# A two-layer graph kernel: its first stage reads edges as joined records, turns the relation weights on TensorE, stores its tables earlier, and lays value and key rows out in 2048 bytes

## The chip, the cores and the metric

The kernel runs on one core of one Trainium2 chip. The metric is the device time of one execution in microseconds (us), lower is better; the number that counts is the median of several runs without the profiler.

## What is computed

Two layers of a graph network over 6250 nodes with 256 features and 200000 edges, sorted by their destination. Cut to what matters here:

```python
# layer 0: attention over the edges of each destination node, 4 heads of 64
enh = x + 0.1 * query_emb
Q, K, V = enh @ Wq + bq, enh @ Wk + bk, enh @ Wv + bv
scores = einsum(Q[dst], K[src] + 0.2 * rel_w[edge_type_64]) / 8      # per head
w = softmax of scores over the edges of each dst
x1 = layernorm(x + layernorm((sum of w * V[src]) @ Wo + bo + x) * gamma + beta)
# layer 1: six relation types
t = einsum('ni,rio->rno', x1, W) + b          # a row for each node and relation
agg[type_6, dst] += t[type_6, src]            # over the edges
out = layernorm(x1 + proj(mean of attention among the 6 rows of a node, + x1))
```

## The kernel before

There are four stages, each one a block of work on all engines, with a barrier behind the first two.

**First stage** (`prepare_phase`). Two things run side by side. TensorE and ScalarE make queries, keys and values for 49 tiles of 128 nodes: SyncE loads a tile of x (L679), TensorE turns it (L562), ScalarE adds the query embedding (L622), TensorE multiplies (L575 queries, L581 keys and values, L589 queries by relation weights), ScalarE copies the results out (L633, L641, L644, L650), SyncE stores the row of keys and values (L686) and the queries (L689), ScalarE's queue stores the relation part (L653). SyncE's queue is in a fixed order: the load of tile i, then the stores of tile i-2. Meanwhile VectorE works out tables of the edges: which edge each row of 128 edges begins with, for layer 0 (14 columns of 128 rows) and for layer 1 (15 columns). For this the edge arrays (src, dst, edge_type_6, edge_type_64) are first copied with padding to arrays in device memory (L666, L671). GpSimd then fetches, for each column, three times 128 rows of 128 numbers (L514, one indirect DMA each for src, dst and the type). TensorE's share of the tables is put between the tiles at fixed half-tile places (`of_tables`, with STARTS, SPREAD, RANGES, ROWS); TensorE waits there for VectorE. After the last tile SyncE's queue stores the tables (L696, L701, L702).

The relation weights are read transposed from device memory, number by number:

```python
for e in range(2):
    eng.dma_start(relc[HD * e:HD * e + HD, :], a["L0_gnn_rel_w"].rearrange("t d -> d t"),
                  allow_slow_non_contiguous=True).then_inc(w_in, 16)
```

A row of keys and values has 514 numbers (2056 bytes): 256 keys, and twice 128 values with a one behind them, whose product with the edge weights gives the softmax's denominator.

**Attention stage** (`attend_phase`). 440 units of 4 x 128 edges. For each, GpSimd gathers 4 x 128 rows of keys and values (L800) into one of 8 buffers; TensorE turns keys (L897), makes scores (L909, L912), turns the exponentials (L919) and sums values (L929). GpSimd waits for L929 of the unit 8 before, to have its buffer free. The indices come from VectorE (L1027), at the stage's start behind a setup of constants (L1099 to L1113).

**Update stage** (`update_phase`). For 49 tiles: the attention's sums and the node's own values are loaded, normalised, multiplied by Wo, added to x, normalised twice, and multiplied by the six relation matrices (L1313).

**Last stage** (`relate_mix_phase`). 1875 gathers of 128 rows of 1024 bytes (L1709), summed by one-hot products (L1740), then the attention among relations.

Of the kernel before, what the change touches and what calls it, by code (L numbers as in the profile page):

```python
# [10 lines left out]
I32 = mybir.dt.int32  # L24

# [9 lines left out]
HEADS = -(-E // 512)  # L35
FAR = 1 << 20
# [6 lines left out]
NQ = NB * P // WQ  # L43
K0 = -(-(E // C0 + NQ + 1) // 8) * 8
VP = 2 * HD + 1
KV = D + 2 * VP
# [63 lines left out]
def prepare_phase(nc, a, t):  # L110


    with ExitStack() as ctx:
        s = Scope(nc, ctx, "pre", give_back=True)
        src1 = s.sb("src1", [P, G1 * P], I32)
        row1 = s.sb("row1", [P, G1 * P])
        keep = s.sb("keep", [P, G1 * P])
        need = s.sb("need", [P, G1 * P], I32)
        ends = s.sb("ends", [P, NW], I32)
# [17 lines left out]
        pad_i = s.sb("pad_i", [2, EPAD - E], I32)  # L137
# [28 lines left out]
        rows_i = s.sb("rows_i", [P, G0, 3, P], I32)  # L166
# [3 lines left out]
        win = s.sb("win", [1, G0 * P])  # L170
        win_i = s.sb("win_i", [1, G0 * P], I32)
# [6 lines left out]
        relc = s.sb("relc", [P, R64])  # L178
# [14 lines left out]
        arrays_padded = s.sem("arrays_padded")  # L193
# [26 lines left out]
        names = ("src", "dst", "edge_type_6", "edge_type_64")  # L220
# [25 lines left out]
        with nc.Block() as block:  # L246
            @block.vector
            def _(eng):
# [50 lines left out]
                def tile_counts(L):  # L299
# [3 lines left out]
                    link(v.tensor_copy(srow[:, 0:P * GB[L]], p_b[:, 0:P * GB[L]]))  # L303
# [82 lines left out]
                def layer0_lists():  # L386
# [8 lines left out]
                    link(v.tensor_scalar(t.rneed0[:, :], win_i[:, :], 2, None, ALU.logical_shift_right))  # L395
                    link(v.tensor_scalar(t.rneed0[:, :], t.rneed0[:, :], 32.0, 32.0, ALU.mult, ALU.add))
# [18 lines left out]
                def make_rows(L, g):  # L415

                    rf = rows_f[g % 2]
                    eng.wait_ge(rows_in[g % G0], 48 * (1 + L + g // G0))
                    link(v.tensor_copy(rf[:, :, :], rows_i[:, g % G0, :, :]))
                    plan["read", L, g] = dve.n  # L420
                    link(v.tensor_scalar(rf[:, 1, :], rf[:, 1, :], rngneg[L][:, g:g + 1], None, ALU.add))
# [7 lines left out]
                    else:  # L429
                        plan["rows", L, g] = dve.n  # L430
                        link(v.tensor_scalar(rf[:, 1, :], rf[:, 1, :], float(WQ), None, ALU.min))
                        plan["rows_b"] = link(v.tensor_copy(rows_b[:, g, :, :], rf[:, 1:3, :]))
# [14 lines left out]
                link(v.memset(pad_i[:, :], 0))  # L447
                plan["pad0"] = link(v.memset(pad_i[0:1, :], FAR))
# [33 lines left out]
            def _(eng):  # L482
                eng.iota(pcol_i[:, :], [[0, 1]], base=0, channel_multiplier=1).then_inc(iota_done, 2)
                eng.iota(t.iota_i[:, :], [[1, IW]], base=0, channel_multiplier=0).then_inc(iota_done, 2)
                for par in range(2):
                    eng.memset(qs[par][:, :, :, :, :], 0.0).then_inc(setup, 1)
                    eng.memset(kv[par][:, :], 1.0).then_inc(setup, 1)
# [1798 lines left out]
```

## Time and profile before

| | |
|---|---|
| median of 3 runs | 5463.11 us (5462.03 to 5466.88) |
| span of the profiled execution, first to last instruction | 7316.7 us |
| first stage in it | 0 to 362 us |
| attention stage in it | 362 to about 3560 us |
| update stage in it | about 3560 to 3945 us |
| last stage in it | about 3945 to 7317 us |
| busy in it: TensorE, VectorE, ScalarE, GpSimd | 78%, 55%, 36%, 51% |
| TensorE's granted clock, mean | 0.89 |

The profiled execution takes 34% longer than a run without the profiler, so its stages can't be subtracted from the median one to one; what a stall in it costs in a plain run has to be argued.

### The profile page before, as it was taken

How to read it: one execution, taken by the hardware profiler on the slowest of the kernel's cores; microseconds unless marked ns; L12 is line 12 of the kernel's file. 1: busy time of each engine (PE TensorE's matmuls, PEld its weight loads, DVE VectorE, ACT ScalarE, POOL GpSimd, SP SyncE). 2: the span in 40 equal slices, each digit the busy share in tenths (PEclk: the TensorE clock that was granted, in tenths of full speed). 3: DMA queues.
4: the chain of work that ended last, by engine and by line, in shares of the span. 5: the costliest groups of instructions: out<-in, count | busy, mean ns of one | idle time of the engine just before them, and what ended most of it. 6: DMA issues, size and time to landing. Idle time of an engine off the chain costs nothing. (4 is left out here: it accounts for less than half of the span.)

```text
span 7316.7 us, 142121 instructions
## 1 busy us (share of the span) xinstructions
PE 5674.8 (78%) x41507; PEld 4231.9 (58%) x41507; DVE 4006.7 (55%) x12046; ACT 2651.7 (36%) x9038; POOL 3696.3 (51%) x3942
## 2 busy tenths in 40 slices
PE   5767777777777777777797688888878788787888
PEld 3356666666666666666553355556656565555666
DVE  4345555555555555555685455555555555555553
ACT  3434444444444444444321133332323233333334
POOL 2255555555555555555344655555555555555550
PEclk8889999989999999998898788888889888889988
DMA  5576666666666666667565444443434434344431
GB/s 137 159 196 172 175 175 172 173 176 175 173 173 175 173 174 174 172 171 166 128 203 163 117 118 118 116 123 108 124 109 121 118 109 122 110 119 119 116 115 34
DMA packets 615779, 1055.40 MB, mean 144 GB/s; under 512 B 150117, under 2 KB 399547, under 8 KB 615504
## 3 DMA queue, kind: packets, MB, share of 16 engines
q0 software_dynamic: 233984, 716.19, 35.8%
q1 hardware_dynamic: 232374, 181.93, 8.3%
q10 hardware_dynamic: 149210, 155.22, 7.3%
q14 instruction: 171, 1.40, 0.1%
q8 instruction: 40, 0.66, 0.0%
HBM read 913.94 MB, written 142.26 MB: 144 GB/s over the span
## 5 line engine op out<-in xcount | busy, mean ns | idle before, releaser
L1709 POOL DMA_INDIRECT rm_xg<-tx_rows,rm_idx x1875 | 1785.1, 952 | 1413.2 <-PE rm_pa L1740 823.1
L800 POOL DMA_INDIRECT at_kv<-kv_rows,at_idx x1760 | 1673.5, 951 | 1559.9 <-PE at_p_o L929 1028.3
L1740 PE MATMUL rm_pa<-rm_xg,rm_oh 128*126 128x256 f32 x3750 | 1246.9, 451 | 557.6 <-DVE rm_acc L2067 435.3
L2067 DVE SCALAR_TENSOR_TENSOR rm_acc<-rm_acc,rm_kp,rm_pa 126x256 f32<-126x256 f32 x1875 | 897.6, 479 | 858.4 <-PE rm_pa L1740 450.0
L1740 PEld LDWEIGHTS rm_pa<-rm_xg,rm_oh 128*126 128x126 f32 x3750 | 711.9, 212 | 942.2 <-DVE rm_acc L2067 526.2
L929 PE MATMUL at_p_o<-at_kv,at_pt 128*64 128x129 f32 x7040 | 750.5, 293 | 630.0 <-issue 549.9
L985 ACT ACTIVATE at_ex<-at_p_s,at_ntop 128x128 f32<-128x128 f32 x1760 | 503.2, 369 | 1377.2 <-DVE at_ntop L1059 1245.0
L929 PEld LDWEIGHTS at_p_o<-at_kv,at_pt 128*64 128x64 f32 x7040 | 491.9, 142 | 854.2 <-issue 838.9
L1051 DVE TENSOR_REDUCE at_cmax<-at_p_s 128x4 f32<-128x512 f32 x440 | 303.8, 690 | 1101.9 <-DMA rows<-pre_rows_b 1055.1
L909 PE MATMUL at_p_s<-at_hot,at_own 128*64 128x128 f32 x7040 | 764.2, 292 | 40.8 <-issue 39.8
L912 PE MATMUL at_p_s<-at_kt,at_own 128*64 128x128 f32 x7040 | 743.0, 283 | 67.1 <-issue 66.7
L1894 ACT ACTIVATE rm_pr<-rm_psc,rm_ntop 126x126 f32<-126x126 f32 x1200 | 422.9, 365 | 842.5 <-DVE rm_ntop L2094 388.8
L1077 DVE SCALAR_TENSOR_TENSOR at_acc<-at_acc,at_fac,at_p_o 128x129 f32<-128x129 f32 x1760 | 611.6, 348 | 93.7 <-remote 31.0
L978 ACT ACTIVATE at_own<-at_rec 128x256 f32 x1760 | 584.5, 404 | 116.2 <-issue 106.7
L897 PE MATMUL at_p_k<-g_ident,at_kv 128*128 128x128 f32 x3520 | 551.6, 309 | 49.4 <-DMA at_kv<-kv_rows,at_idx 34.0
L1752 PE MATMUL rm_pq<-rm_xt,rm_wt 128*128 128x504 f32 x1200 | 570.2, 598 | 5.8 <-issue 5.8
L2086 DVE TENSOR_REDUCE rm_top<-rm_psc 126x2 f32<-126x252 f32 x600 | 223.4, 414 | 614.3 <-remote 413.5
L909 PEld LDWEIGHTS at_p_s<-at_hot,at_own 128*64 128x64 f32 x7040 | 457.4, 144 | 140.3 <-issue 138.1
L912 PEld LDWEIGHTS at_p_s<-at_kt,at_own 128*64 128x64 f32 x7040 | 487.6, 144 | 84.6 <-issue 84.5
L897 PEld LDWEIGHTS at_p_k<-g_ident,at_kv 128*128 128x128 f32 x3520 | 485.5, 163 | 54.4 <-issue 50.6
L961 ACT ACTIVATE at_kt<-at_p_k,at_bk 128x512 f32<-128x512 f32 x440 | 304.4, 692 | 334.9 <-DMA pre_rows_i<-pad_edge_type,pre_e0i 155.8
L2057 DVE TENSOR_SCALAR rm_oh<-g_iota,rm_rw 128x126 f32<-128x126 f32 x1875 | 403.5, 290 | 0.0
(250 smaller groups left out, 7364.4 us busy)
## 6 DMA issues: line engine op xcount, KB each, us to landing
at_row<-rows ACTq DMA_DIRECT2D x440, 128.0 KB
agg_rows<-rm_acc SPq DMA_DIRECT2D x300, 126.0 KB
rm_st<-agg_rows ACTq DMA_DIRECT2D x75, 504.0 KB
rm_srow<-agg_rows ACTq DMA_DIRECT2D x75, 504.0 KB
tx_rows<-up_tx SPq DMA_DIRECT2D x49, 768.0 KB, 3.6
rm_xg<-tx_rows,rm_idx POOLq DMA_INDIRECT x1875
at_kv<-kv_rows,at_idx POOLq DMA_INDIRECT x1760
sums<-at_acc SPq DMA_DIRECT2D x196, 64.5 KB
```

The costliest lines, as they stand in the source:

```text
L800: eng.indirect_dma_start(out=kv[j][:, c, :], out_offset=None, in_=t.kv, in_offset=bass.IndirectOffsetOnAxis(ap=idx[:, o:o + 1], axis=0),). ...
L897: mm = eng.transpose(p_k[k][:, c * P:c * P + P], kv[j][:, c, P * k:P * k + P], t.ident[:, :])
L909: eng.matmul(p_s[j % 2][64 * k:64 * k + 64, at], own[:, o, P + 64 * k:P + 64 * k + 64], hot[j % 2][:, at], start=True, stop=False)
L912: mm = eng.matmul(p_s[j % 2][64 * k:64 * k + 64, at], own[:, o, 64 * k:64 * k + 64], kt[j % 2][:, k, c, :], start=False, stop=True)
L929: mm = eng.matmul(p_o[b][64 * k:64 * k + 64, VE * (c % 2):VE * (c % 2) + VE], pt[j % 2][:, c, 64 * k:64 * k + 64], kv[j][:, c, D + VE * k: ...
L978: ins = act(own[:, o, :], rec[:, bass.ds(held["slots"][k], 1), :].rearrange("p a c -> p (a c)"), ACT.Copy)
L985: ins = act(ex[j % 4][:, c, :], p_s[j % 2][:, P * c:P * c + P], ACT.Exp, bias=ntop[j % 2][:, c:c + 1])
L1077: v.scalar_tensor_tensor(acc[:, o, :], acc[:, (o - 1) % ACCS, :], fac[j % 4][:, c:c + 1], p_o[c // 2][:, VE * (c % 2):VE * (c % 2) + VE], ...
L1709: eng.indirect_dma_start(out=xg[:, q % XR, :], out_offset=None, in_=t.tx, in_offset=bass.IndirectOffsetOnAxis(ap=idx[:, q % IR:q % IR + 1] ...
L1740: eng.matmul(p_a[q % BANKS][0:WR, 0:D], oh[:, q % OR, :], xg[:, q % XR, :], start=True, stop=True).then_inc(summed, 1)
L1752: mm = eng.matmul(p_q[:, 0:QP], wt[:, k, c, :], xt[piece][:, k, :], start=(k == 0), stop=(k == 1))
L2067: v_.scalar_tensor_tensor(acc[:, q % AR, :], acc[:, (q - 1) % AR, :], kp[0:WR, q % AR:q % AR + 1], p_a[q % BANKS][0:WR, 0:D], ALU.mult, AL ...
```

## The change

- The four edge arrays are no longer copied to four padded arrays. Only dst is, for the look-up of starts. All four are loaded to the chip's memory as 125 partitions of 1600 numbers each, GpSimd writes them interleaved (four copies), and one array `edges` of records of four numbers is stored to device memory (again 125 partitions), with its padding. The records' order is edge_type_64, src, dst, edge_type_6, so that a layer's three numbers lie together.
- GpSimd fetches one row of 128 records (2048 bytes) for each column of rows in place of three rows of 512 bytes.
- SyncE's queue gets the loads of the edge arrays behind the first two loads of x, and the store of `edges` behind the load of tile 5, with a wait for GpSimd's copies; the stores of the tables move from the end to a place behind the load of tile 46.
- VectorE does `starts(1)` before `tile_counts(0)`, and waits for the store of `edges` before it sorts the units; TensorE's places for tables move.
- The relation weights are loaded in rows (64 x 64, twice side by side), turned by TensorE and scaled by ScalarE.
- A row of keys and values has 512 numbers (2048 bytes): values of heads 0 and 1, keys, values of heads 2 and 3. ScalarE copies it with one instruction in place of three. The ones stand in the attention stage's buffers, set once at its start; the gathered row is written between them.
- In the attention stage the first indices are copied before the constants are set.
- In the update stage a tile's sums come with one DMA (2064 bytes a row) in place of two, and its own values with one in place of two.
- Several lists of counts are of 16 bits.

```diff
+EP = 125
+EW = E // EP
 VP = 2 * HD + 1
-KV = D + 2 * VP
+KV = 2 * D
+KVW = KV + 32
+VAT, KAT = (15, 400), 144
...
 # vector, first stage
                 starts(0)
+                starts(1)
                 tile_counts(0)
                 first_edges(0)
-                starts(1)
                 tile_counts(1)
+                eng.wait_ge(edges_out, 32)
                 sort_units()
...
 # gpsimd, first stage
-                eng.wait_ge(arrays_padded, 16 * 8)
+                eng.wait_ge(dst_padded, 32)
...
+                for k in range(4):
+                    eng.wait_ge(arrays_in, 16 * 4)
+                    eng.tensor_copy(joined[:, :, k], plain[:, k, :]).then_inc(joined_done, 1)
...
-                        for k, name in enumerate(("src", "dst", ("edge_type_64", "edge_type_6")[L])):
-                            eng.indirect_dma_start(
-                                out=rows_i[:, g % G0, k, :], out_offset=None,
-                                in_=t.pads[name].rearrange("(r c) -> r c", c=1),
-                                in_offset=bass.IndirectOffsetOnAxis(ap=e0i[L][:, g:g + 1], axis=0),
-                            ).then_inc(rows_in[g % G0], 16)
+                        eng.indirect_dma_start(
+                            out=rows_i[:, g % G0, :, :].rearrange("p e k -> p (e k)"), out_offset=None,
+                            in_=t.edges, in_offset=bass.IndirectOffsetOnAxis(ap=e0i[L][:, g:g + 1], axis=0),
+                        ).then_inc(rows_in[g % G0], 16)
...
 # tensor, first stage
-                STARTS, SPREAD, RANGES, ROWS = (6, 18), 22, (36, 63), (46, 72)
+                STARTS, SPREAD, RANGES, ROWS = (9, 10), 23, (36, 66), (47, 75)
...
+                eng.transpose(p_r[0][:, 0:R64], relr[:, :, :].rearrange("t e d -> t (e d)"), t.ident[0:R64, 0:R64]
+                              ).then_inc(rel_ps, 1)
...
 # sync, first stage
+                load(0, 0, True, P)
+                load(1, 1, True, P)
+                join_edges()
+                for i in range(2, 6):
+                    load(i, i % 2, False, P)
+                eng.wait_ge(joined_done, 4)
+                eng.dma_start(t.edges[0:E, :].rearrange("(p e) k -> p (e k)", p=EP), shared[0:EP, :]
+                              ).then_inc(edges_out, 16)
+                with eng.Fori(3, NB // 2 - 1) as k:
+                    load(k * 2, 0, False, P)
+                    load(k * 2 + 1, 1, False, P)
+                load(NB - 3, 0, False, P)
+                store_tables()
+                load(NB - 2, 1, False, P)
+                load(NB - 1, 0, False, N - (NB - 1) * P)
...
 # gpsimd, attention stage
-                            out=kv[j][:, c, :], out_offset=None, in_=t.kv,
+                            out=kv[j][:, c, 16:16 + KV], out_offset=None, in_=t.kv,
...
 # vector, attention stage
+                for b in range(2):
+                    set_rows(2 * b, b)
...
+                for i in range(U):
+                    v.memset(kv[i][:, :, VAT[0]:VAT[0] + 1], 1.0)
+                    ins = v.memset(kv[i][:, :, VAT[1] + VE - 1:VAT[1] + VE], 1.0)
```

## Rows read from the trace of the kernel before

**Rows 1.** Windows: a stretch, its length, busy us by engine, clock, DMA share, GB/s.
```profile
360.00:3560.00 3200.00, 2415.41 (x26112) 1978.39 (x26112) 1833.49 (x4910) 1381.58 (x4355) 1673.53 (x1760) 0.91 0.64 174
3600.00:3900.00 300.00, 290.82 (x888) 153.06 (x889) 233.63 (x821) 73.45 (x231) 135.38 (x187) 0.96 0.63 189
```
**Rows 2.** Groups by shape, 600 to 3400 us: the gather, and the matmul that waits for it.
```profile
L800 POOL DMA_INDIRECT at_kv<-kv_rows,at_idx x1543 | 1466.7, 951 | 1332.9 <-PE at_p_o L929 912.4 <-issue 380.5 <-remote 37.9
L897 PE MATMUL at_p_k<-g_ident,at_kv 128*128 128x128 f32 x3080 | 482.6, 309 | 0.4 <-issue 0.4
```
**Rows 3.** Timeline of the start: start us, length, engine (q: its queue), line, work.
```profile
4.89 13.22 ACTq L614 DMA_DIRECT2D pre_relc<-in_L_gnn_rel_w_dram  x2
22.01 0.22 POOL L490 TENSOR_SCALAR pre_qcol<-pre_qcol 128x2 f32<-128x2 f32 x1 [18.78 <-DMA pre_relc<-in_L_gnn_rel_w_dram]
22.97 0.66 PE L562 MATMUL pre_pt<-g_ident,pre_x 128*128 128x128 f32 x2 [14.02 <-POOL pre_rel L492]
```
**Rows 4.** Timeline, SyncE's queue: stores of tiles 0, 6, 9, 21, 29 and 48.
```profile
31.65 0.23 SPq L686 DMA_DIRECT2D kv_rows<-pre_kv  x1
...
61.91 0.02 SPq L686 DMA_DIRECT2D kv_rows<-pre_kv  x1
...
123.26 0.33 SPq L686 DMA_DIRECT2D kv_rows<-pre_kv  x1
...
182.54 0.33 SPq L686 DMA_DIRECT2D kv_rows<-pre_kv  x1
...
249.04 0.27 SPq L686 DMA_DIRECT2D kv_rows<-pre_kv  x1
...
344.77 0.33 SPq L686 DMA_DIRECT2D kv_rows<-pre_kv  x1
```
**Rows 5.** Timeline, GpSimd: first and last gather of rows, each layer (42 and 45).
```profile
60.60 1.01 POOL L514 DMA_INDIRECT pre_rows_i<-pad_src,pre_e0i  x1 [27.49 <-DVE pre_e0i L359]
...
112.24 0.95 POOL L514 DMA_INDIRECT pre_rows_i<-pad_edge_type,pre_e0i  x1 [0.30 <-issue]
184.60 0.98 POOL L514 DMA_INDIRECT pre_rows_i<-pad_src,pre_e0i  x1 [71.41 <-DVE pre_rows_f L431]
...
275.56 0.95 POOL L514 DMA_INDIRECT pre_rows_i<-pad_edge_type,pre_e0i  x1 [0.30 <-issue]
```
**Rows 6.** DMA, 68 to 118 us: GB/s in 40 slices.
```profile
GB/s 211 100 264 124 85 162 52 59 52 52 49 56 52 52 52 53 52 52 52 52 52 52 61 232 72 56 52 207 104 56 157 53 56 154 23 49 56 30 0 0
```
**Rows 7.** Timeline: TensorE's turn of the last tile, of 106 rows.
```profile
327.71 0.38 SPq L679 DMA_DIRECT2D pre_x<-in_x_dram  x1
...
334.19 0.69 PE L562 MATMUL pre_pt<-g_ident,pre_x 128*128 128x128 f32 x2 [3.28 <-DMA pre_x<-in_x_dram]
```
**Rows 8.** Timeline: the same of a tile of 128 rows.
```profile
314.67 0.41 SPq L679 DMA_DIRECT2D pre_x<-in_x_dram  x1
...
318.09 0.44 PE L562 MATMUL pre_pt<-g_ident,pre_x 128*128 128x128 f32 x2 [0.67 <-DMA pre_x<-in_x_dram]
```
**Rows 9.** Timeline: the last of nine table stores, and the next stage's start.
```profile
356.46 1.06 SPq L702 DMA_DIRECT2D tables<-pre_ubase  x1
...
362.04 0.15 DVE L1099 TENSOR_SCALAR at_half<-g_col 128x1 f32<-128x1 f32 x1 [47.38 <-PEq L90]
366.39 0.95 POOL L800 DMA_INDIRECT at_kv<-kv_rows,at_idx  x1 [43.20 <-DVE at_idx L1027]
```
**Rows 10.** DMA, 345 to 362 us: all packets.
```profile
DMA packets 5001, 4.54 MB, mean 267 GB/s; under 512 B 3717, under 2 KB 4487, under 8 KB 5000
```
**Rows 11.** GpSimd: a set of 3584 numbers (timeline), an addition of 256 (lines, 3600 to 3900).
```profile
22.81 3.09 POOL L493 MEMSET g_fresh<- 128x3584 f32 x1
...
L1248 POOL TENSOR_TENSOR up_yg<-up_y,g_gamma 128x256 f32<-128x256 f32 x47 | 34.4, 731 | 144.3 <-DVE up_y L1424 144.3
```
**Rows 12.** DMA, GpSimd's queue: 600 to 3400 us, then 4200 to 7200 us.
```profile
q0 software_dynamic: 123378, 405.98, 53.2%
...
q0 software_dynamic: 82063, 224.17, 26.2%
```

More of the change, by code:

```diff
@@ L24 @@
 I32 = mybir.dt.int32
+U16 = mybir.dt.uint16
 P = 128
@@ L35 @@
 HEADS = -(-E // 512)
+PADS = 64
+PADW = (EPAD - E) // PADS
+assert PADS * PADW == EPAD - E
 FAR = 1 << 20
@@ L690, in store, with join_edges @@
                                   qs[par][:, :, :, :, :].rearrange("p w k e n -> p w (k e n)")).then_inc(out_q[par], 16)
-                each(eng, load)
+                def join_edges():
+                    for k, name in enumerate(names):
+                        eng.dma_start(plain[:, k, :], a[name].rearrange("(p e) -> p e", p=EP)).then_inc(arrays_in, 16)
+                    eng.wait_ge(dve.sem, plan["pad_e"])
+                    eng.dma_start(t.edges[E:EPAD, :].rearrange("(p e) k -> p (e k)", p=PADS),
+                                  pad_e[:, :, :].rearrange("p e k -> p (e k)")).then_inc(edges_out, 16)
@@ new lines, in store_tables @@
+                def store_tables():
+                    eng.wait_ge(dve.sem, plan["rows_b"])
+                    for k in range(2):
+                        eng.dma_start(t.rows0[k, :].rearrange("(g p e) -> p g e", p=P, e=C0),
+                                      rows_b[:, :, k, :]).then_inc(rows0_out, 16)
+                    eng.wait_ge(dve.sem, plan["taken", 1, G1 - 1])
+                    for k, of in enumerate((src1, row1, keep, need, ends, slot)):
+                        rows = P if k < 3 else 1
+                        eng.dma_start(t.tables1[k][0:rows, :], of[0:rows, :]).then_inc(tables_out, 16)
+                    eng.dma_start(t.tables1[6][:, :], ubase[:, :, :].rearrange("p u e -> p (u e)")
+                                  ).then_inc(tables_out, 16)
@@ L698, in _ @@
-                eng.wait_ge(dve.sem, plan["taken", 1, G1 - 1])
-                for k, of in enumerate((src1, row1, keep, need, ends, slot)):
-                    rows = P if k < 3 else 1
-                    eng.dma_start(t.tables1[k][0:rows, :], of[0:rows, :]).then_inc(tables_out, 16)
-                eng.dma_start(t.tables1[6][:, :], ubase[:, :, :].rearrange("p u e -> p (u e)")).then_inc(tables_out, 16)
                 for par in range(2):
@@ L720, in attend_phase @@
         FLOOR = -float(2 ** 90)
-        kv = [s.sb(f"kv{i}", [P, CH, KV]) for i in range(U)]
+        kv = [s.sb(f"kv{i}", [P, CH, KVW]) for i in range(U)]
         idx = s.sb("idx", [P, U * CH], I32)
@@ L1135, in update_phase @@
         zero = s.sb("zero", [P, D])
-        sums = [s.sb(f"sums{i}", [P, 2 * (VP + 3)]) for i in range(R)]
+        sums = [s.sb(f"sums{i}", [P, 2 * MASS]) for i in range(R)]
         xb = [s.sb(f"xb{i}", [P, D]) for i in range(R)]
```

190 lines of the change are left out of this document (95 added, 95 removed).

## The prediction

> **What bounds the kernel now.** I read the windows by stage first. In the attention stage TensorE is busy for 2415 of 3200 us and GpSimd for 1674; in the update stage TensorE for 291 of 300 [rows 1]. The groups of the attention stage come next: GpSimd's gathers wait 912 us for a buffer that L929 frees, while TensorE's first use of gathered rows waits 0.4 us in 2800 [rows 2]. So in the profiled run the attention stage goes by TensorE's instructions, and a row that arrives sooner is not late for anything. The gather itself holds GpSimd for 951 ns, with 0.30 us to the next where nothing holds it [rows 5], so four of them take 5.0 us; a unit takes 3200/440 = 7.3 us in the trace, and 3200/440 x 5463/7317 = 5.4 us if the plain run is shorter everywhere by the same share. That is close to GpSimd's own pace, which does not depend on the row's width: rows of 512 bytes [rows 5] take as long as those of 2056 [rows 2].
>
> Then the timeline of the first stage, by SyncE's stores, one for each tile. Three things stand out. First, TensorE turns its first tile only at 22.97 us, since the relation weights are read number by number: their two DMAs hold ScalarE's queue for 13.22 us, and GpSimd's scaling waits until 22.01 [rows 3]. Second, tiles take 4.94 us each in a quiet stretch (9 to 21: (182.54 - 123.26)/12), but tiles 6 to 9 take 61.4 us in place of 14.8, and tiles 21 to 29 take 66.5 in place of 39.5 [rows 4]: 46.5 + 27.0 = 73.5 us lost. These are the two stretches in which GpSimd gathers edge rows, 42 and 45 times [rows 5]. In the first, the rate in most slices is 52 GB/s, which is the gathers alone (64 KB in 1.25 us), while the loads and stores of SyncE and ScalarE go in short bursts [rows 6]. Third, from the last tile's store at 344.77 to the next stage at 362.04 only tables are stored [rows 4, 9].
>
> **The change part by part.** The sum is made against the profiled execution's 7316.7 us; the median is 5463.1. Tiles of the first stage are paced by few and long instructions and by DMAs, so I take its microseconds over to the plain run one for one. That is a choice, and the third case below is what happens if it fails.
>
> *Relation weights.* The DMAs that read them become rows as the other weights are, so the gate opens when the plain loads have landed. SyncE's queue has one copy of an edge array before the first x in place of four. ScalarE's other loads are issued by 4.89 us [rows 3]; with two short issues and a landing of 3.4 us as a load of x needs [rows 8], the first turn comes at about 9.5: -13.5 us. The added turn and the scaling are one instruction each, beside waiting engines: nothing. If the load in two pieces lands late it is -8, and -16 at most.
>
> *Joining the edges.* New on SyncE's queue: four loads of 0.8 MB behind the second x, and a store of 3.2 MB behind tile 5's. Behind them in the same queue stand x 2 and x 6, and whatever the queue stores later. Large transfers run at 267 GB/s [rows 10], so 3.2 MB is 12 us if all goes well. It may not, with 125 partitions: the one load whose count of rows has few divisors, 106, is turned 6.5 us after its issue [rows 7], one of 128 rows after 3.4 [rows 8], which is twice the time for less data. I take twice: 24 us. Then the loads, issued at 7, land at 31; x 2 is wanted at 19 (9.5 + the 8.7 us from the first turn to the first store [rows 3, 4]) and comes at 32: 13 us. GpSimd's four copies of 1600 numbers are bounded by an addition of 256 in 731 ns, 4.6 us each, and by a set of 3584 in 3.09 us, 1.4 us each [rows 11]; at 3 us between, they end at 43. The store goes out at 44 and is through at 68. x 6, behind it, is wanted about three tiles after x 2, at 48: 21 us. Together +34. At full rate it would be 8; at a fifth of the full rate (60 us each) about 106. Layer 0's gathers then start when `edges` has landed, 68 us in place of 60.6; TensorE first wants their rows at half-tile 47, far behind, so that costs nothing.
>
> By the Trainium skill ("DMA: Bandwidth & Descriptors", section on why a DMA increments its semaphore by 16) a transfer from SyncE runs on the largest number of DMA engines up to 16 that divides its slowest dimension: 5 for 125 rows, 2 for 106. The rows of the 106-row load agree in direction. By that rule the transfers take 16/5 of 12 us, the two waits about 63 us together, and the kernel ends 29 us later than in my sum; it is the mechanism of the fourth case.
>
> *Gathers of records.* 87 become 29. The first flood was 42 x 1.25 = 52.5 us long and cost 46.5; 14 x 1.25 = 17.5 us would cost 15.5 at the same share. The second cost 27.0 with 45 gathers; 15 gathers, each waiting for a reading of layer 0's rows every half tile, cost 9. So 73.5 become 24.5: -49 us. Each gather now moves four times the bytes, which may starve the others more while it lasts; as much as before in all would be 0 saved, and no stall at all -73.5. VectorE reads the records with a stride, at the same count of numbers, and has half of its time free.
>
> *Key and value copy.* One copy in place of three on ScalarE, which is not late in a tile: nothing.
>
> *Tables earlier.* Behind the last tile there is left one store to land (3.4 us) in place of 17.3: -14. But the nine issues, 12 us, now stand before x 47, which is then 12 + 3.4 us behind, and is wanted 4.9 us later: +10.5. Net -3; from -14, if the load is not held, to 0.
>
> *Attention stage.* Indices come before the constants: the first gather at about 363 in place of 366.39 [rows 9], -3. The 16 small sets of ones stand behind it, while rows are on their way. The gathered row is 8 bytes shorter; TensorE doesn't wait for it: nothing in the likeliest case. GpSimd issues as many gathers as before.
>
> *Update stage.* Fewer and longer pieces for sums and own values, 130 KB more a tile, in a stage in which TensorE is busy 97%: nothing, within 3 us.
>
> The sum: -13.5 + 34 - 49 - 3 - 3 = -34.5 us, so 7282 for the profiled execution, and **5428.6** for the median, taken as 5428.
>
> **The rivals.**
>
> *The shorter row matters in the attention stage, chance 0.18.* In the plain run the stage goes faster and DMA may be what holds it. The trace has 0.64 of the DMA engines' time in it [rows 1]; at 5.4 us a unit in place of 7.3 that is 0.87. The price of a row: 53.2% of 16 engines over 2800 us for 1543 x 128 rows is 121 ns for 2056 bytes; 26.2% over 3000 us for 224.17 MB in rows of 1024 is 57.4 ns, so 115 for 2048 [rows 2, 12]. If the odd 8 bytes cost that difference, 5%, and the stage (about 2390 us in a plain run) goes by DMA, it gains up to 115 us: 5313, and half of it 5371. Against it: TensorE waits 0.4 us for the rows.
>
> By the same page's section on how a descriptor splits into AXI transactions, a piece that does not start at a multiple of 256 bytes costs up to a further transaction. Rows of 2056 bytes start at such a multiple only now and then, those of 2048 in device memory always. That speaks for this case, and I give it no more for it, since the wait is not there.
>
> *My sum, chance 0.56*, 5385 to 5450 by its terms' bounds.
>
> *The floods don't stall the plain run, chance 0.16.* Then the records save nothing: -34.5 + 49 = +14.5, or 5478; with the joins at full rate (8 in place of 34) -11.5, or 5452. For it: the profiled run is 34% longer as a whole, so some of its stalls are its own. Against it: the bursts are in the data that DMA moves, not in instructions.
>
> *The joins cost more than the floods give back, chance 0.10.* The waits for x 2 and x 6 are 34 in my sum; from 68.5 us on, with transfers at about a quarter of the full rate, the change is slower. At a fifth it is 106 - 34 = 72 more: 5500.
>
> **How the numbers follow.** The likeliest gives 5428. The range leaves out the outer half of the first rival and most of the last: 5345 to 5475; the likeliest case's own is 5385 to 5450. About 11 us, 0.2%, is what a measurement can tell. Faster: 0.18 + 0.54 of the 0.56 + 0.04 of the third = 0.76. Same: 0.02 + 0.07 + 0.02 = 0.11. Slower: 0.05 + 0.08 = 0.13.
>
> **What would show it.** In the trace after: the first turn at about 9.5 us; a gap before the turn of tile 2 of about 13 us and before tile 6 of about 21, both ended by the load of x; 14 gathers that end within 20 us, and tiles around them that take 5 to 8 us each; a gap of some 10 us before the turn of tile 47; the attention stage at about 331 us in place of 362 and as long as before. I am wrong if the attention stage's length changes by over 1% in the windows, if layer 0's gathers stall the tiles as long as they did, or if a table wait of TensorE (VectorE held by `edges_out`) ends later than the loads.

## The result, and the profile after

The changed kernel takes 5514.25 us (median of 4 runs, 5511.41 to 5524.31) against 5462.57 us for the old one on the same chip: ratio 1.0097, 95% interval [1.0083, 1.0111]. It is slower by about 52 us, where 5428 had been forecast.

The windows of the changed kernel by stage (first stage, attention, update, last stage); the columns are those of [rows 1]:

```profile
0.00:326.28 326.28, 228.26 (x955) 126.51 (x955) 149.50 (x445) 156.67 (x395) 49.66 (x51) 0.89 0.59 182
326.28:2619.80 2293.52, 1983.01 (x26400) 1766.40 (x26400) 1834.93 (x4989) 1398.78 (x4400) 1673.62 (x1760) 0.96 0.85 242
2619.80:2975.10 355.30, 327.34 (x980) 170.01 (x980) 254.29 (x885) 79.52 (x246) 141.57 (x196) 0.94 0.57 197
2975.10:5509.60 2534.50, 2364.60 (x13173) 1786.81 (x13173) 1749.35 (x5744) 1023.03 (x3900) 1782.93 (x1878) 0.96 0.53 150
```

The first thing to see is the span: 5509.6 us, 1.8 us under the time of that execution. This profile is as long as a plain run, and the old kernel's is not. So the two can't be set side by side stage by stage; what the old first stage does in a plain run had to be measured anew (the second experiment below gives it: 290.7 us, where [rows 9] have the next stage at 362).

The timeline of the changed kernel's start, SyncE's queue, the turns of tiles 0, 2 and 6, and GpSimd's joining:

```profile
7.33 0.34 SPq L703 DMA_DIRECT2D pre_rows_i<-in_edge_type_dram  x1
...
9.05 11.65 SPq L705 DMA_DIRECT2D edges<-pre_pad_e  x1
...
11.62 0.69 PE L571 MATMUL pre_pt<-g_ident,pre_x 128*128 128x128 f32 x2 [0.23 <-POOL pre_bq L499]
...
21.56 2.64 SPq L694 DMA_DIRECT2D kv_rows<-pre_kv  x1
41.88 11.80 POOL L511 COPY pre_shared<-pre_rows_i 125x1600 int32<-125x1600 int32 x4 [22.30 <-DMA pre_rows_i<-in_edge_type_dram]
...
42.26 0.69 PE L571 MATMUL pre_pt<-g_ident,pre_x 128*128 128x128 f32 x2 [22.91 <-DMA pre_x<-in_x_dram]
48.79 0.33 SPq L694 DMA_DIRECT2D kv_rows<-pre_kv  x1
...
58.74 0.46 SPq L727 DMA_DIRECT2D edges<-pre_shared  x1
62.76 0.36 SPq L694 DMA_DIRECT2D kv_rows<-pre_kv  x1
...
88.92 0.99 POOL L524 DMA_INDIRECT pre_rows_i<-edges,pre_e0i  x1 [32.10 <-DMA edges<-pre_shared]
...
89.42 0.69 PE L571 MATMUL pre_pt<-g_ident,pre_x 128*128 128x128 f32 x2 [26.08 <-DMA pre_x<-in_x_dram]
...
94.89 0.34 SPq L694 DMA_DIRECT2D kv_rows<-pre_kv  x1
```

Both waits that the prediction named are there, each ended by the load of x: 22.9 us before tile 2 and 26.1 before tile 6. Each stands behind about 3.2 MB: the arrays are issued from 7.33 us and in at 41.88, 34.6 us later; the records are issued at 58.74 and GpSimd's first gather of them is let go at 88.92, 30.2 us later. How busy the DMA engines are meanwhile, 62 to 86 us, in 40 slices (each digit is the busy share in tenths):

```profile
DMA  4257896855542424333334243243333342423422
```

From the middle on the digits are 2 to 4, about three tenths of 16 engines, while nothing but the records is under way.

The same kernel at the end of the first stage:

```profile
290.16 0.34 SPq L694 DMA_DIRECT2D kv_rows<-pre_kv  x1
...
291.05 2.79 SPq L712 DMA_DIRECT2D rows<-pre_rows_b  x2
...
303.23 0.65 SPq L718 DMA_DIRECT2D tables<-pre_ubase  x1
305.05 0.36 SPq L694 DMA_DIRECT2D kv_rows<-pre_kv  x1
...
307.80 0.69 PE L571 MATMUL pre_pt<-g_ident,pre_x 128*128 128x128 f32 x2 [13.48 <-DMA pre_x<-in_x_dram]
...
321.14 0.33 SPq L694 DMA_DIRECT2D kv_rows<-pre_kv  x1
326.28 0.39 SPq L843 DMA_DIRECT2D at_bk<-in_L_gnn_bk_dram  x1
```

### The profile page after: what moved, and what is told of

Same layout as the page of the kernel before. It is cut to its first block and busy times, and to the rows that moved or that the text cites. A ratio compares the mean times of both kernels' runs of the same rounds, so it can differ in the third digit from the quotient of the medians.

```text
span 5509.6 us, 141658 instructions
## 1 busy us (share of the span) xinstructions
PE 4903.2 (89%) x41508; PEld 3849.7 (70%) x41508; DVE 3988.1 (72%) x12063; ACT 2658.0 (48%) x8941; POOL 3647.8 (66%) x3885
## 5 line engine op out<-in xcount | busy, mean ns | idle before, releaser
L1777 PE MATMUL rm_pa<-rm_xg,rm_oh 128*126 128x256 f32 x3750 | 1063.6, 408 | 130.6 <-DVE rm_acc L2104 75.7
L1777 PEld LDWEIGHTS rm_pa<-rm_xg,rm_oh 128*126 128x126 f32 x3750 | 677.3, 195 | 397.0 <-issue 167.9
L943 PE MATMUL at_p_s<-at_hot,at_own 128*64 128x128 f32 x7040 | 735.7, 287 | 22.8 <-ACT at_own L1012 19.8
L931 PE MATMUL at_p_k<-g_ident,at_kv 128*128 128x128 f32 x3520 | 483.1, 282 | 282.8 <-DMA at_kv<-kv_rows,at_idx 242.3
L946 PE MATMUL at_p_s<-at_kt,at_own 128*64 128x128 f32 x7040 | 712.0, 280 | 0.0
L931 PEld LDWEIGHTS at_p_k<-g_ident,at_kv 128*128 128x128 f32 x3520 | 401.3, 144 | 324.2 <-issue 242.5
L943 PEld LDWEIGHTS at_p_s<-at_hot,at_own 128*64 128x64 f32 x7040 | 444.5, 142 | 102.9 <-issue 94.7
L963 PE MATMUL at_p_o<-at_kv,at_pt 128*64 128x129 f32 x7040 | 472.6, 276 | 7.5 <-DVE at_pt L1078 7.1
L946 PEld LDWEIGHTS at_p_s<-at_kt,at_own 128*64 128x64 f32 x7040 | 469.7, 142 | 0.0
L963 PEld LDWEIGHTS at_p_o<-at_kv,at_pt 128*64 128x64 f32 x7040 | 399.1, 138 | 26.5 <-issue 16.2
```

Source lines behind the costliest of these rows:

```text
L931: mm = eng.transpose(p_k[k][:, c * P:c * P + P], kv[j][:, c, KAT + P * k:KAT + P * k + P], t.ident[:, :])
L943: eng.matmul(p_s[j % 2][64 * k:64 * k + 64, at], own[:, o, P + 64 * k:P + 64 * k + 64], hot[j % 2][:, at], start=True, stop=False)
L946: mm = eng.matmul(p_s[j % 2][64 * k:64 * k + 64, at], own[:, o, 64 * k:64 * k + 64], kt[j % 2][:, k, c, :], start=False, stop=True)
L963: mm = eng.matmul(p_o[b][64 * k:64 * k + 64, VE * (c % 2):VE * (c % 2) + VE], pt[j % 2][:, c, 64 * k:64 * k + 64], kv[j][:, c, VAT[k]:VAT[ ...
L1777: eng.matmul(p_a[q % BANKS][0:WR, 0:D], oh[:, q % OR, :], xg[:, q % XR, :], start=True, stop=True).then_inc(summed, 1)
```

## The experiments

Ratios are to the old kernel on the same chip; the ratios can be compared with each other, the medians of different chips not, since the old kernel's own median was 5461 to 5482 on the chips used. "16-bit lists" means that the lists need, ends, rneed0 and ends0 have 16-bit numbers, as in the changed kernel.

**Large transfers in pieces of 112 and 13 partitions**, the rest as changed:

```
+for lo, hi in ((0, 112), (112, EP)):
+    eng.dma_start(plain[lo:hi, k, :], a[name].rearrange("(p e) -> p e", p=EP)[lo:hi, :]).then_inc(arrays_in, 16)
...
+for lo, hi in ((0, 112), (112, EP)):
+    eng.dma_start(t.edges[0:E, :].rearrange("(p e) k -> p (e k)", p=EP)[lo:hi, :], shared[lo:hi, :]).then_inc(edges_out, 16)
```

> The changed kernel with the loads of the edge arrays and the store of the records each split in two: partitions 0 to 111 and 112 to 124, so that the large part's count of rows is a multiple of 16. If the transfers of 125 rows are slow because few DMA engines carry them (theory 1): the loads, issued at 8 us, land by about 22 in place of 42, and the store, issued at about 40, by 55 in place of 89; the waits before tiles 2 and 6 fall from 23 + 26 us to about 5 + 8, and the kernel takes about 5478. If the transfers take as long on 16 engines (bounded by device memory or by GpSimd's copies, theory 2): both waits stay within 5 us of 23 and 26 and the time stays at 5514.

Measured: 5492.69 us against 5460.95, ratio 1.0062 [1.0045, 1.0079]. The first stage takes 298.1 us in place of 326.3. Its DMA from 44 to 62 us, in which the records go out:

```profile
DMA  0007998994984949495997967949992222111236
```

Most digits are 7 to 9 where they were 3, and they fall after some 27 slices of 0.45 us, 12 us in place of 30. TensorE's waits before tiles 2 and 6 fall to 9.4 and 12.9 us, nearer to theory 1's 5 and 8 than to theory 2's 23 and 26. So the transfers of 125 partitions ran on a part of the DMA engines. That was 24.5 us of the loss by the gaps between the stores of tiles 0 and 1 and of tiles 4 and 5 (59.3 us together in the changed kernel, 34.8 here), and some 20 by the medians. (The first stage as a whole is 28 us shorter, but two runs with the same code in it differ by up to 4.5 us: 326.3 and 321.8 in the changed kernel and in the one with its ones set by GpSimd below.)

**The old kernel with 16-bit lists and nothing else.**

```
-need = s.sb("need", [P, G1 * P], I32)
+need = s.sb("need", [P, G1 * P], U16)
```

> The kernel before with one part of the change alone, the lists of counts in 16 bits (as in the changed kernel). It also gives a profile of the old first stage that is as long as a plain run. Every theory expects 5461 +- 5 us. If the first stage alone is to blame (theory 1): attention, update and last stage are as long as in the changed kernel within 5 us, and the first stage ends at about 270 to 280 us in place of the 362 of the long profile, with the tiles stalled by under 20 us in all while GpSimd gathers edge rows. If a later stage is to blame (theory 2): the first stage ends at 310 us or later and a later stage is at least 20 us shorter than in the changed kernel.

Measured: ratio 0.9999 [0.999, 1.0008], and a profile whose span, 5463.6 us, is that of a plain run (it was the shortest of its 11 runs, whose median on that chip is 5480.56, the old kernel's own being 5481.67). It stands for the old kernel from here on. Windows by stage:

```profile
0.00:290.73 290.73, 221.59 (x954) 121.71 (x954) 146.93 (x444) 158.99 (x492) 95.80 (x108) 0.97 0.68 185
290.73:2597.40 2306.67, 1993.32 (x26400) 1773.73 (x26400) 1834.75 (x4973) 1396.11 (x4400) 1673.86 (x1760) 0.96 0.88 242
2597.40:2954.46 357.06, 329.18 (x980) 170.73 (x980) 258.82 (x885) 79.47 (x246) 142.40 (x197) 0.94 0.58 178
2954.46:5463.60 2509.14, 2354.04 (x13173) 1780.34 (x13173) 1748.44 (x5744) 1023.20 (x3900) 1785.78 (x1878) 0.96 0.53 152
```

And SyncE's stores of tiles 0, 1, 4, 5, 44 and 48, with the start of the next stage:

```profile
33.07 0.36 SPq L688 DMA_DIRECT2D kv_rows<-pre_kv  x1
...
37.46 0.34 SPq L688 DMA_DIRECT2D kv_rows<-pre_kv  x1
...
53.05 0.33 SPq L688 DMA_DIRECT2D kv_rows<-pre_kv  x1
...
57.95 0.33 SPq L688 DMA_DIRECT2D kv_rows<-pre_kv  x1
...
252.91 0.34 SPq L688 DMA_DIRECT2D kv_rows<-pre_kv  x1
...
273.59 0.33 SPq L688 DMA_DIRECT2D kv_rows<-pre_kv  x1
...
290.73 0.41 SPq L810 DMA_DIRECT2D at_bk<-in_L_gnn_bk_dram  x1
```

GpSimd's 42 gathers for layer 0 begin at 61.77 us and its 45 for layer 1 are done by 206; the 42 are 1.25 us apart as in [rows 5], and the tiles go on at 5 us through them. Tiles 5 to 44 take 195.0 us here with 87 gathers, and 195.3 in the changed kernel (94.89 to 290.16) with 29. The stalls of [rows 4] are not in this profile, which is as long as a plain run.

Stage by stage the changed kernel against this one: first stage +35.6 us, attention -13.2, update -1.8, last stage +25.4; together +46.0, the difference of the spans. (The medians on one chip differ by 52; two single profiles are compared here.)

**The new rows alone:** 16-bit lists, rows of 2048 bytes, the attention and update stages as changed; edge arrays, gathers, tables and relation weights as before.

```
-KV = D + 2 * VP
+KV = 2 * D
...
-act(kv[par][:, 0:D], p_kv[par][:, 0:D], ACT.Copy).then_inc(kv_done, 1)
+act(kv[par][:, :], p_kv[par][:, :], ACT.Copy).then_inc(kv_done, 1)
```

> The kernel of the run before this one, with rows of 2048 bytes, the attention stage and the update stage of the changed kernel, and the old first stage otherwise (old gathers of edges, old padded copies, old read of the relation weights, tables stored at the end). Theory 1 (first stage to blame): 5455 to 5461, so no change or the 3 us of the earlier indices. Theory 2 (the new rows and layouts cost): 5480 or more. If the shorter row helps after all: 5440 or less.

Measured: ratio 1.002 [1.0011, 1.0029], slower. First stage 285.3 us, attention 2308.9, update 359.1, last stage 2535.6. The first stage is shorter than the old kernel's with its three copies of keys and values for a tile: tiles 5 to 44 take 190.0 us, with all 87 gathers. The last stage reads none of these rows and its code is unchanged, and yet it takes 26 us more than in the old kernel. The waits show where. VectorE's and TensorE's waits in 2000 us of the last stage, first the old kernel with 16-bit lists:

```profile
DVE rm_top L2088 <- issue: 47.4, 21, 2.7
...
PE rm_pa L1742 <- DVE rm_acc L2069: 45.9, 39, 2.3
```

then this one (line numbers one higher):

```profile
PE rm_pa L1743 <- DVE rm_acc L2070: 66.0, 43, 3.2
...
DVE rm_acc L2070 <- issue: 19.6, 21, 1.4
```

"Issue" is a halt for which the profile shows no releaser. In the old kernel VectorE has one such halt in each pass of the last stage's loop (21 in 2000 us, 2.3 us each). The new one has a second, 0.9 us each, and TensorE waits 20 us more for the accumulated rows. In the changed kernel it is 41 further halts and 28.5 us, the second one at the same place and a third of 0.3 us elsewhere in the pass:

```profile
PE rm_pa L1777 <- DVE rm_acc L2104: 66.6, 42, 3.6
...
DVE rm_acc L2104 <- issue: 28.5, 41, 1.5
```

**The ones set by GpSimd.** The attention stage now sets the columns of ones itself, with 16 instructions on VectorE ahead of its loop. Here they are GpSimd's; the rest is as in the run before.

```
+eng.memset(kv[i][:, :, VAT[0]:VAT[0] + 1], 1.0)
...
-v.memset(kv[i][:, :, VAT[0]:VAT[0] + 1], 1.0)
```

> The kernel of the run with the new key and value rows alone (its last stage took 2535 us in the profile, against 2509 with the old rows), with one edit: the 16 small sets of ones are GpSimd's, so that VectorE's stream of instructions is as long ahead of the last stage as in the old kernel. Theory A, place in the stream: the last stage's loop begins 16 instructions later in VectorE's stream, and a second halt with no releaser (about 0.9 us, 21 times in 2000 us) stands behind the one at the turn of its loop; it goes, TensorE's waits for the accumulated rows fall from 66 to about 46 us, and the last stage takes 2509 us again. Theory B, the narrower rows: device memory behind them lies 50,176 bytes lower, or the attention stage leaves the clock or the queues otherwise; then the last stage stays at 2535.

Measured: ratio 0.9977 [0.9967, 0.9987], faster than the old kernel; last stage 2511.5 us, the second halt gone, TensorE's wait for the accumulated rows 46.6 us. The loss was in those 16 instructions.

**16 and 128 empty instructions at the end of VectorE's first stage**, in the old kernel with 16-bit lists:

```
+for k in range(16):
+    v.memset(idle[:, k:k + 1], 0.0)
```

> The old kernel with 16-bit lists and 16 empty instructions (sets of one number) at the end of VectorE's first stage, where it waits some 46 us. Theory A, place in the stream: the last stage takes 2535 us in place of 2509, with the second halt behind the turn of the loop, and the time is 10 to 25 us above that of the same kernel without them. Theory B, rows and memory: no change, since neither is touched.

> As the run before, with 128 empty instructions. Theory A: the halts of VectorE in the last stage stand at other instructions of its loop; whether they cost more or less is not known beforehand, from 15 us less than the old kernel to 50 us more, and the attention stage may move too. Theory B: no change beyond the 128 instructions themselves, which lie in a wait of 46 us: within 5 us.

Measured: 1.0002 [0.9993, 1.0011] and 1.0007 [0.9998, 1.0016]; last stage 2508.4 and 2511.9 us. No second halt. Instructions ahead in the stream are not enough by themselves; why not is open.

**Two parts of the change alone: the relation weights turned on TensorE, and the early indices.**

```
+eng.dma_start(relr[:, e, :], a["L0_gnn_rel_w"]).then_inc(w_in, 16)
...
+eng.transpose(p_r[0][:, 0:R64], relr[:, :, :].rearrange("t e d -> t (e d)"), t.ident[0:R64, 0:R64]).then_inc(rel_ps, 1)
```

> The old kernel with 16-bit lists and two parts of the change alone: the relation weights read as rows and turned on TensorE, and the attention stage's first indices set ahead of its constants. If my two terms stand (13.5 and 3 us in the prediction), the first store comes at 21 us in place of 33, the first gather of the attention stage 3 us earlier, and the time is 14 to 16 us below that of the old kernel: 0.25 to 0.3%. Rival: what is gained at the start is given back before the attention stage, where the lists of edges and not the tiles end last; then the gain is under 5 us.

Measured: ratio 0.9971 [0.9962, 0.9981]. The first stage ends at 282.3 us, 8.4 earlier; the first turn is at 18.32 us and now waits for the load of x behind the copies of the edge arrays. The attention stage's first gather begins 1.1 us after the stage, where it was 4.4, but the stage takes 2308.5 us: the early indices give nothing that shows in its length.

**16 empty instructions at the head of VectorE's attention stage**, where the ones are set in the changed kernel; the rest is the old kernel with 16-bit lists:

```
+for k in range(16):
+    v.memset(idle[:, k:k + 1], 0.0)
 v.tensor_scalar(half[:, :], t.col[:, 0:1], float(R64), ...
```

> The old kernel with 16-bit lists and 16 empty instructions of VectorE at the head of its attention stage, just where the new kernel sets its ones. In the run with the new rows alone the last stage took 2535 us; with the ones set by GpSimd 2511.5; with 16 empty instructions at the end of the first stage 2508. Theory A, place in the stream, counted from the head of the attention stage (what stands in the first stage is made up for before): the second halt in the last stage's loop comes back and that stage takes 2535 us, the time is some 20 us above the old one. Theory C, the sets themselves or the new rows together with them: the last stage stays at 2509 and the time within 5 us of the old one.

Measured: ratio 1.0049 [1.0035, 1.0062], last stage 2532.8 us. Sixteen sets of one number, which take 59 ns each and nobody waits for, cost 25 us in a stage that begins some 2660 us later. The turn of VectorE's loop in the last stage, without them (the old kernel with 16-bit lists):

```profile
3312.93 0.75 DVE L2088 TENSOR_REDUCE rm_top<-rm_psc 126x2 f32<-126x252 f32 x2 [2.66 <-issue]
...
3314.40 2.23 DVE L2069 SCALAR_TENSOR_TENSOR rm_acc<-rm_acc,rm_kp,rm_pa 126x256 f32<-126x256 f32 x4
```

and with them:

```profile
3313.52 0.75 DVE L2091 TENSOR_REDUCE rm_top<-rm_psc 126x2 f32<-126x252 f32 x2 [2.25 <-issue]
...
3315.72 2.23 DVE L2072 SCALAR_TENSOR_TENSOR rm_acc<-rm_acc,rm_kp,rm_pa 126x256 f32<-126x256 f32 x4 [0.80 <-issue]
```

After the halt at the turn there are five instructions, and then a second halt of 0.80 us that the other stream doesn't have.

The traces also say what the halts go with. Their DMA part has packets of a kind of its own, "instruction". On the page of the old kernel with 16-bit lists:

```profile
q14 instruction: 171, 1.40, 0.1%
```

These are packets of 8192 bytes, and they are rare: one in 17 us of the last stage. Yet at each of the 21 turns in that kernel one starts within 0.2 us before and 0.6 us after the beginning of the halt, and a next one 2.4 to 3.2 us later, for which VectorE doesn't halt. In this run each of the 21 second halts comes behind that next packet, which starts 0.4 to 1.1 us ahead of the halt and 1.8 to 2.0 us before work goes on (at 3313.95 us for the halt shown). So VectorE halts at the turn while code is fetched, and the second halt fits instructions behind the turn that run out before the next piece has come.

**8 and 64 empty instructions in the same place.**

> The old kernel with 16-bit lists and 8 empty instructions at the head of VectorE's attention stage, where 16 made the last stage 25 us longer (2533 in place of 2509). If the halt depends on where the loop's head falls among the pieces in which code is fetched, 8 may or may not do it: 2509 or 2533, and nothing between. If the halt grows with the count of instructions, 2521.

> As the run before with 64 empty instructions. If the place of the loop's head counts, the halt behind its turn may be gone again: 2509 in the last stage. If it grows with the count, or if each instruction there costs, 2533 or more.

Measured: 0.9996 [0.9986, 1.0006] and 1.0003 [0.9994, 1.0013]; last stage 2512.6 and 2515.6 us, with one halt each pass and 44.5 and 46.2 us of TensorE's waits. So 0, 8 and 64 don't do it and 16 does (2532.8 to 2535.6 us in the five kernels that have 16 there, 2507.9 to 2515.6 in the ten others): not a cost that grows with instructions, but a place.

**The changed kernel with the ones set by GpSimd.**

> The changed kernel with the 16 sets of ones on GpSimd in place of VectorE. If they are all that lengthens the last stage (A or C), it takes 2510 us in place of 2534.5, and the time is 5492 on the chip of the first comparison, 0.5% above the old one; what is left of the loss is the first stage's 35.6 us less what the attention stage gives (some 10). If the last stage stays at 2534 the halt is tied to something else of the new first stage.

Measured: ratio 1.0049 [1.0035, 1.0063] in place of 1.0097; first stage 321.8 us, attention 2297.3, update 356.2, last stage 2515.0. Half of the loss was the place.

**Edge arrays loaded from ScalarE's queue, records stored from GpSimd's**, with the pieces of 112 and 13 partitions and the ones on GpSimd:

```
 # scalar, first stage, behind the weights
+eng.dma_start(plain[lo:hi, k, :], a[name].rearrange("(p e) -> p e", p=EP)[lo:hi, :]).then_inc(arrays_in, 16)
 # gpsimd, behind its four copies
+eng.dma_start(t.edges[0:E, :].rearrange("(p e) k -> p (e k)", p=EP)[lo:hi, :], shared[lo:hi, :]).then_inc(records_out, 16)
```

> The changed kernel with its large transfers in pieces of 112 and 13 partitions, ones set by GpSimd, and one more edit: the edge arrays are loaded from ScalarE's queue and the records are stored from GpSimd's, so that no load of x stands behind them in SyncE's queue. With them in SyncE's queue the stores of tiles 0 to 1 were 15.1 us apart and those of 4 to 5 19.7, against 4.4 and 4.9 in the old first stage: 25 us. Theory Q, the order in the queue: both gaps fall under 8 us, and the first stage takes about 277 us in place of 298. Theory D, the DMA engines themselves, each working off what was issued before: the gaps stay within 5 us of what they were and the first stage takes 293 us or more, since the loads of x find the engines taken.

Measured: ratio 1.0001 [0.9992, 1.001], first stage 294.5 us. The stores of tiles 0 to 1 are 12.2 us apart and those of 4 to 5 18.1 (15.1 and 19.7 with all in SyncE's queue, 4.4 and 4.9 in the old kernel). Of the 25 us that remained in these two gaps 4.5 went. A load of x from another queue gets ahead of the arrays, but not by much. First this run, then the one with all in SyncE's queue:

```profile
25.16 0.69 PE L578 MATMUL pre_pt<-g_ident,pre_x 128*128 128x128 f32 x2 [5.66 <-DMA pre_x<-in_x_dram]
...
28.97 12.52 POOL L513 COPY pre_shared<-pre_rows_i 125x1600 int32<-125x1600 int32 x4 [9.66 <-DMA pre_rows_i<-in_edge_type_dram]
```

```profile
28.67 12.52 POOL L511 COPY pre_shared<-pre_rows_i 125x1600 int32<-125x1600 int32 x4 [9.40 <-DMA pre_rows_i<-in_edge_type_dram]
...
30.40 0.69 PE L571 MATMUL pre_pt<-g_ident,pre_x 128*128 128x128 f32 x2 [9.37 <-DMA pre_x<-in_x_dram]
```

Issued at about 13.3 us in both, x 2 is turned 11.8 us later with a queue of its own and 17.1 without, where [rows 8] have 3.4; from 13.3 us until that turn the engines are busy all the time in both. So the rest is most likely that the DMA engines are taken, whichever queue the transfer came from.

**The tables stored last again**, the rest as changed:

```
-store_tables()
 load(NB - 2, 1, False, P)
 load(NB - 1, 0, False, N - (NB - 1) * P)
 store(NB - 2, 1)
 store(NB - 1, 0)
+store_tables()
```

> The changed kernel with the nine stores of the tables back behind the last tile. By the gaps in its profile the early stores cost 10.3 us before the turn of the third last tile but one and saved 12 behind the last. If these are what moving them does, the first stage takes 328 us in place of 326.3 and the time does not move by more than 3 us from the changed kernel's. If the wait is longer than the stores' own time because they fill the DMA engines, moving them back gains up to 5 us.

Measured: ratio 1.0108 [1.0091, 1.0124], which can't be told from 1.0097; first stage 324.6 us against 326.3. In the two gaps themselves the early stores save a little: from the store of tile 44 to the next stage it is 37.2 us here and 36.1 in the changed kernel. 1 us can't be seen in the whole.

**The parts that pay, without the others:** new rows, ones on GpSimd, relation weights turned on TensorE, early indices; edge arrays, 87 gathers and late tables as in the old kernel.

> The parts of the change that paid, without the others: new rows of 2048 bytes with the attention and update stages of the changed kernel, ones set by GpSimd, relation weights as rows and turned on TensorE; the edge arrays, the 87 gathers and the late tables stay as in the old kernel. The two parts alone gave 0.9977 (rows, with ones on GpSimd) and 0.9971 (relation weights and early indices). If they add up the ratio is about 0.995 to 0.996, 22 to 27 us below the old time: first stage about 279 us, attention 2300, update 356, last 2510. If the attention stage is paced by GpSimd's gathers alone and the gain of the rows was chance, 0.997.

Measured: 5447.55 us against 5466.40, ratio 0.9964 [0.9951, 0.9978]: first stage 279.5 us, attention 2295.5, update 355.8, last stage 2514.7. It beats both kernels, by 19 us the old one. That is less than expected: the two parts alone, 0.9977 and 0.9971, multiply to 0.9948.

## Why the prediction was wrong, point by point

The predicted sum was -34.5 us. The measured one, from the two profiles that are as long as a plain run, is +46.0. Two steps failed: stalls that only the long profile has were taken for stalls of the kernel, and the 16 sets of ones were put at nothing.

**The choice that failed** stands ahead of the sum: the microseconds of the first stage of a profile that was 34% longer than a plain run were taken over one for one. The third rival said what follows if that fails, and it did fail. That rival's own figure is 5478; with the joins as they turned out it is 5492.

*Gathers of records, -49 predicted, 0 measured.* The failed step is "73.5 become 24.5". The old kernel's floods cost a run of plain length nothing that shows (195.0 against 195.3 us for tiles 5 to 44), so there was nothing to save. The argument "the bursts are in the data that DMA moves, not in instructions" was no evidence: it showed that the long profile's stalls were real in that profile, not that a plain run has them.

*Key and value copy, 0 predicted.* The comparison just made has this copy in it too. With 87 gathers tiles 5 to 44 take 194.0 to 198.0 us with the old rows (7 kernels) and 188.5 to 190.5 with the new ones (3 kernels), so the new rows, written with one copy in place of three, save some 5 us here. With the new rows and 29 gathers they take 190.5 to 195.3 (5 kernels), some 4 us more than with 87: the fewer and longer gathers save nothing and may cost a little.

*Joining, +34 predicted, +48.4 measured.* Stores of tiles 0 to 4 take 41.2 us against 20.0, and of 4 to 5 32.1 against 4.9. The mechanism and both places were right; the size was too small by 14, since "twice the time for less data" stood for the factor: 24 us were reckoned for each transfer, the arrays took 34.6 and the records 30.2. (At full rate the prediction's own steps give 10 us and not 8.) By the Trainium skill ("DMA: Bandwidth & Descriptors", section on why a DMA increments its semaphore by 16) 125 rows go to 5 of the 16 engines. The trace agrees: three tenths of them are busy, 5/16 is 0.31, and pieces of 112 partitions raise it to 7 to 9 tenths. The prediction quoted the rule and kept it out of the sum. Its 63 us for the two waits is too much: the records went at 106 GB/s (3.2 MB in 30.2 us) and the arrays at 93, where 5/16 of 267 is 83.

*Relation weights, -13.5 predicted.* The first store is at 21.56 us in place of 33.07: -11.5. The first turn is at 11.62 where 9.5 was forecast. Alone, with the copies of the edge arrays still ahead of x in the queue, it gives 8.4 by the first stage's length.

*Tables, -3 predicted* (-14 + 10.5 is -3.5). From the store of tile 44 to that of 48 30.98 us against 20.68, so +10.3 (10.5 had been forecast, and its place was right); from there to the next stage 5.1 us against 17.1, so -12.0 where -14 stood. The net is -1.7 against the old kernel and -1.1 against the run with the tables last again. That this run's first stage is 1.7 us shorter as a whole is less than the 4.5 us by which the same code differs.

*Attention stage, -3 predicted.* Measured -13.2 in these two profiles; over all of them the old rows give 2304 to 2312 us (7 kernels) and the new ones 2294 to 2309 (8 kernels), means 2307.2 and 2299.1: some 8 us. What bounds the stage in a plain run is neither what the prediction read in [rows 2] nor what the first rival says. GpSimd's queue of DMA and GpSimd's waits, 600 to 2400 us, old kernel with 16-bit lists:

```profile
q0 software_dynamic: 114724, 377.49, 73.4%
```

```profile
POOL at_kv L802 <- issue: 403.4, 1324, 0.3
```

and the changed kernel:

```profile
q0 software_dynamic: 114681, 375.90, 70.0%
```

```profile
POOL at_kv L835 <- issue: 409.1, 1343, 0.3
```

The row is cheaper, as the rival reckoned: 16 x 1800 us x 0.734 over 1433 x 128 rows is 115 ns, and with 0.700 and 1435 gathers 110 ns, 5% less. (The rival had the difference right and both prices 5 ns high; the queue's packets are fewer than its rows.) But GpSimd issues gathers all the time, 1433 and 1435 of them at 951 ns with 0.30 between, which is 1.79 of 1.80 ms. The DMA engines have 12 and 16% free, so cheaper rows hardly make it faster: from the stage's 100th gather to its 1600th it takes 1883 to 1890 us with the old rows and 1882 to 1889 with the new ones. The 8 us lie outside that stretch, and what they are is not shown. TensorE is not the bound: it waits 170 us (old) and 180 us (changed) for the rows in that stretch of 1800 us, where [rows 2] had 0.4 in 2800:

```profile
PE at_p_k L899 <- DMA at_kv<-kv_rows,at_idx: 169.7, 120, 5.0
```

The prediction had come close in its first paragraph, with 5.0 us for four gathers and 5.4 for a unit, but kept the long profile's wait as the bound.

*Update stage, 0 predicted:* 355.3 against 357.1 us; right.

*Last stage, not in the sum at all: +25.4.* This is half of the loss. It comes from the 16 sets of ones, which the prediction costed at nothing since they stand "behind" the first gather. That they cost the attention stage nothing was right; that they move the code of VectorE behind them was not thought of. Shown: the halt comes with 16 instructions there (the ones or empty ones), goes when they are GpSimd's, isn't there with 0, 8 or 64, stands five instructions behind the turn of the loop, and comes each time behind a packet of instructions. By the Trainium skill ("Runtime: NRT & Kernel Launch", section "Instruction fetch mechanics") code is fetched in blocks of 256 instructions, and a taken branch out of what is held forces a fetch. The halt at each turn of the loop agrees with that, with a packet of instructions at each of the 21; the packets that come with VectorE's halts have 8192 bytes, and no run here shows how many of them make a block. A second halt just behind fits a head that lies a few instructions ahead of a block's end; that the head lies there is argued from the place of the halt, not read from an address. Why 16 instructions in the first stage don't do it is open (room left between the stages' code would explain it).

**Range and chances.** The range ended at 5475 and the result is 5514, 39 us outside. Of these 25 are the last stage, for which no case stood; without it the result would be 5489, still 14 outside. The rest is the third case (0.16) together with a join term that was 14 us too small. The fourth case (0.10) did not come true by its own condition, 68.5 us of waits where 48.4 were measured. Floods that cost nothing and slow joins can both be so, and should not have been treated as exclusive. The two together with the Trainium skill's rule for the joins, quoted above, would have given 5507, near the result by luck: the rule's price was 15 us too high, and the last stage was not in it.

## What to carry to other kernels

Before a stall is priced, compare the profile's span with the plain run: where it is a third longer, stalls in it are not yet stalls of the kernel, and a harmless edit that yields a profile as long as a plain run is the cheapest first step. Split a large transfer so that its main part has a count of partitions that 16 divides (112 of 125 here), and ask what small loads are wanted while it runs, on any queue. When a stage with unchanged code and data gets longer, look for halts without a releaser at the turn of its loops and for packets of instructions beside them, and move a few instructions to another engine or pad them before redesigning anything.

## What the runs showed of the hardware

A transfer of 125 partitions kept three tenths of the 16 DMA engines busy and took 30.2 us for 3.2 MB; in pieces of 112 and 13 the engines were 7 to 9 tenths busy. A load of 128 KB from another queue came only partly past such a transfer: turned 11.8 us after its issue in place of 17.1, with 3.4 where nothing is in the way; of 25 us of waits 4.5 went with the change of queue.

A loop of some 95 us on VectorE halts 2.2 us on average at each turn (1.8 to 2.9), beside a packet of 8192 bytes of instructions, and 1.0 us more (0.7 to 1.3) five instructions later if its head falls in the wrong place (21 passes of the run with 16 empty instructions). TensorE, which is 97% busy there, lost somewhat more than the halts themselves: 19.9 us of halts in 2000, and 1.2% fewer matmuls (11022 against 11157), which is 24 us of 2000, at a granted clock of 0.98 in place of 0.99. The old kernel with 16-bit lists:

```profile
3204.00:5204.00 2000.00, 1940.55 (x11157) 1481.47 (x11157) 1475.37 (x4857) 868.67 (x3306) 1515.07 (x1593) 0.99 0.57 160
```

and the same with 16 empty instructions at the head of the attention stage:

```profile
3203.00:5203.00 2000.00, 1930.26 (x11022) 1472.67 (x11022) 1453.91 (x4796) 857.99 (x3265) 1506.15 (x1582) 0.98 0.55 159
```
